# Value products of a fused attention layer: which loop stands innermost

## The reference

```python
q, k, v = split(x @ Wqkv + bqkv)              # 16 heads of 16 channels
scores[.., i] = q[n] . k[n - OFFSETS[i]] * scale + pos_bias[i]
alpha = softmax(scores over the offsets 0..32, 48, 64, 96, 128, 192, 256, 384)
out[n] = sum_i alpha[n, i] * v[n - OFFSETS[i]]
x = layernorm(x + (out * sigmoid(x @ Wgate + bgate)) @ Wout + bout)
```

## Time and profile before

| | before |
|---|---|
| runs, us | 1961.47, 1965.34, 1973.05 |
| median, us | 1965.34 |
| profiled execution, from first to last instruction, us | 1999.0 |
| TensorE busy | 1512.8 us (76%) |
| VectorE, ScalarE, GpSimd busy | 989.1, 905.2, 708.5 us |
| mean granted TensorE clock | 0.797 of full speed |

### The profile page before, as it was taken

One profiled execution on the slowest core, in us unless ns is written; L12 is line 12 of the kernel. 1 busy time (PEld: TensorE's weight loads), 2 busy tenths in 40 slices (PEclk: granted clock), 3 DMA queues, 4 the chain that ended last, 5 costly groups with the idle time before them and its releaser, 6 DMA issues. The chain is left out here.

```text
span 1999.0 us, 72320 instructions
## 1 busy us (share of the span) xinstructions
PE 1512.8 (76%) x31232; PEld 1001.5 (50%) x31232; DVE 989.1 (49%) x2117; ACT 905.2 (45%) x1544; POOL 708.5 (35%) x654
## 2 busy tenths in 40 slices
PE   2447777887778787877778787887875499999970
PEld 1235554555554554545555555555643266776660
DVE  5214455454554455455545455554645355555525
ACT  3123353444435353435445353545443366656626
POOL 6022233433334253333334252433323113323335
PEclk9566786868777797878778787878766699999995
DMA  4483453535243443525242433525210424443328
GB/s 120 91 227 93 88 105 81 112 90 111 76 102 79 88 104 79 116 77 112 64 105 73 88 92 68 110 72 110 57 47 14 140 75 91 101 105 87 72 30 339
DMA packets 220103, 194.55 MB, mean 97 GB/s; under 512 B 66847, under 2 KB 207151, under 8 KB 219648
## 3 DMA queue, kind: packets, MB, share of 16 engines
q1 hardware_dynamic: 204464, 175.11, 35.3%
q0 software_dynamic: 15360, 15.10, 4.7%
HBM read 98.07 MB, written 86.18 MB: 92 GB/s over the span
## 5 line engine op out<-in xcount | busy, mean ns | idle before, releaser
L396 POOL TENSOR_TENSOR p<-p 128x512 f16<-128x512 f32 x96 | 129.0, 1344 | 440.5 <-ACT p L796 427.4
L810 ACT COPY featT<-gp 128x1024 f16<-128x1024 f16 x96 | 93.4, 1032 | 321.3 <-PE gp L541 321.3
L396 DVE TENSOR_TENSOR p<-p 128x512 f16<-128x512 f32 x96 | 94.7, 987 | 284.7 <-ACT p L796 282.8
L548 PE MATMUL gp<-featT,wr 128*128 128x512 f16 x768 | 209.4, 432 | 22.8 <-DVE mT L959 13.8
L1107 POOL DMA_INDIRECT disp<-y,sidx x128 | 174.1, 1360 | 53.6 <-issue 38.0
L1364 POOL DMA_INDIRECT xln<-y,place x64 | 104.9, 1639 | 216.0 <-DVE y L1506 175.7
L1402 PE MATMUL up<-rowsT,w 128*128 128x512 f16 x768 | 171.3, 383 | 9.6 <-DVE w L1479 6.1
L1416 PE MATMUL dn<-w,h 128*128 128x256 f16 x1536 | 170.1, 273 | 0.0
L623 PE MATMUL o<-v_near,p 128*32 128x66 f16 x2048 | 132.3, 203 | 40.0 <-issue 28.4
L795 ACT ACTIVATE p<-st 128x512 f16<-128x512 f32 x192 | 116.7, 608 | 101.0 <-PE st L592 98.1
L1416 PEld LDWEIGHTS dn<-w,h 128*128 128x128 f16 x1536 | 149.7, 98 | 17.3
(11 more groups left out here) (176 smaller groups left out, 3127.0 us busy)
## 6 DMA issues: line engine op xcount, KB each, us to landing
qk_dram<-qk SPq DMA_DIRECT2D x64, 256.0 KB, 2.5
v_near<-vs SPq DMA_DIRECT2D x224, 66.0 KB
qs<-qk_dram SPq DMA_DIRECT2D x96, 128.0 KB, 4.4
ks<-qk_dram SPq DMA_DIRECT2D x96, 128.0 KB, 7.4
o_dram<-o_far SPq DMA_DIRECT2D x64, 136.0 KB, 5.7
o_back<-o_dram SPq DMA_DIRECT2D x16, 544.0 KB, 4.3
v_dram<-vs SPq DMA_DIRECT2D x16, 528.0 KB
v_far<-v_dram SPq DMA_DIRECT2D x64, 132.0 KB
```

The costliest lines, as they stand in the source:

```text
L396: engine.tensor_tensor(p16[:, b, 1, :], p32[:, b, :], p16[:, b, 0, :], ALU.subtract).then_inc(is_split, 1)
L548: last = nc.tensor.matmul(dst, lhs(a, c), rhs(b, c), start=(k == 0), stop=(k == len(todo) - 1))
L810: gp_done(nc.scalar.copy(featT[:, i, :, :].rearrange("f c t -> f (c t)"), bank[:, :].bitcast(F16)), n, stage, PART_OF_T[stage], i)
```

## The change

The loops of the value products are turned inside out: for a pair of heads (z, e) and a term (high or low part of p, with its columns of v), the innermost loop now runs over the four groups of 32 output partitions (near) or over the eight blocks, which are the four groups in each of the two banks (far). Each product keeps its operands, its columns, its bank and its flags, and on one group of partitions the terms of one (z, e) still follow one another in the same order. The count of instructions, the waits at the head and the increment behind the last product stay.

```diff
-                terms3 = ((0, slice(0, OW)), (0, slice(OW, VW)), (1, slice(0, OW)))
-                blocks = [(r8, r8 % 4, 2, 256) for r8 in range(8)] if k < FAR_PAIRS else [(b, b, 4, P) for b in range(4)]
-                for blk, b, groups, width in blocks:
...
-                    for z in range(groups):
                         for e in range(2):
...
-                                nc.tensor.matmul(dst, p(0), v, start=True, stop=False, skip_group_check=True)
-                                last = nc.tensor.matmul(dst[:, :, 0:OW], p(1), v[:, :, 0:OW], start=False, stop=True, skip_group_check=True)
...
+                p = lambda e, a, c: p16[:, 2 * (k % 2) + e, a, c:c + BLOCK]
+                if k < FAR_PAIRS:
+                    for z in range(2):
                         for e in range(2):
+                            for j, (a, cols) in enumerate(((0, slice(0, OW)), (0, slice(OW, VW)), (1, slice(0, OW)))):
+                                for r8 in range(8):
+                                    quad = slice(BLOCK * (r8 % 4), BLOCK * (r8 % 4 + 1))
...
+                                    last = nc.tensor.matmul(dst, p(e, a, 256 * z + BLOCK * r8), v, start=(j == 0), stop=(j == 2), skip_group_check=True)
+                else:
+                    for z in range(4):
+                        for e in range(2):
+                            for a, width in ((0, VW), (1, OW)):
+                                for b in range(4):
+                                    quad = slice(BLOCK * b, BLOCK * (b + 1))
...
+                                    last = nc.tensor.matmul(dst, p(e, a, P * z + BLOCK * b), v, start=(a == 0), stop=(a == 1), skip_group_check=True)
```

More of the change, by code:

```diff
@@ L610, in values @@
                     alone.wait_ge(v_near_in, n.at(256, 256))
-                terms3 = ((0, slice(0, OW)), (0, slice(OW, VW)), (1, slice(0, OW)))
-                blocks = [(r8, r8 % 4, 2, 256) for r8 in range(8)] if k < FAR_PAIRS else [(b, b, 4, P) for b in range(4)]
-                for blk, b, groups, width in blocks:
-                    quad = slice(BLOCK * b, BLOCK * (b + 1))
-                    far = k < FAR_PAIRS
-                    for z in range(groups):
-                        for e in range(2):
[L618 to L622, removed]
-                                nc.tensor.matmul(dst, p(0), v, start=True, stop=False, skip_group_check=True)
-                                last = nc.tensor.matmul(dst[:, :, 0:OW], p(1), v[:, :, 0:OW], start=False, stop=True, skip_group_check=True)
[L625 to L630, removed]
@@ new lines, in values @@
+                p = lambda e, a, c: p16[:, 2 * (k % 2) + e, a, c:c + BLOCK]
+                if k < FAR_PAIRS:
+                    for z in range(2):
+                        for e in range(2):
+                            for j, (a, cols) in enumerate(((0, slice(0, OW)), (0, slice(OW, VW)), (1, slice(0, OW)))):
+                                for r8 in range(8):
+                                    quad = slice(BLOCK * (r8 % 4), BLOCK * (r8 % 4 + 1))
+                                    v = v_far[:, 8 * k + r8, :, :, 2 * z + e, cols].rearrange("p u v c -> p (u v) c")
+                                    dst = o[r8 // 4][:, 0:H * OW].rearrange("q (w h c) -> q w h c", w=4, c=OW)[quad, :, 2 * z + e, 0:cols.stop - cols.start]
+                                    last = nc.tensor.matmul(dst, p(e, a, 256 * z + BLOCK * r8), v, start=(j == 0), stop=(j == 2), skip_group_check=True)
[5 more added lines that the diff above has]
+                                    quad = slice(BLOCK * b, BLOCK * (b + 1))
+                                    v = v_near[:, 4 * (k - FAR_PAIRS) + b, :, 2 * z + e, 0:width]
+                                    dst = o[e][:, 0:PAIRS * VW].rearrange("q (u z c) -> q u z c", u=2, c=VW)[quad, :, z, 0:width]
+                                    last = nc.tensor.matmul(dst, p(e, a, P * z + BLOCK * b), v, start=(a == 0), stop=(a == 1), skip_group_check=True)
```

## The result

The kernel after takes 1944.58 us in the median of eight runs (1936.55 to 1954.96), the kernel before 1962.77 us beside it (eight runs, 1958.3 to 1973.05): ratio 0.9895, 95% interval 0.9866 to 0.9924. It is faster, as forecast and clear of noise, but by 18 us (1%) where 60 were forecast.

What follows compares the result with a forecast made beforehand. TensorE's own order of work was taken to bound a batch. Terms 2.0 + 0 + 1.3 + 0.2 + 0.7 = 4.2 us a batch, 62 us in all, scaled and rounded to 60: 1905 us; range 1860 to 1956.

Steps and rivals of the forecast that it cites:

- The price of a unit: Value products on TensorE: with four groups at once, 8 ns a product, far units 0.88 us, near 0.62, unit 3 0.85.
- the seams: Where one output group's products give way to the next in a unit, they run side by side, 17.5 ns each.
- No overlap: Rival: four interleaved groups don't overlap, or instructions can't come faster than 25 ns a product; 1965 us, chance 0.08.
- two at a time: Lower bound for value units: 17.5 ns a product as at the seams, saving 0.4 us near, 0.7 far.
- Units 0 and 1: Far value products, slots 2 and 4: 3.2 us saved on TensorE, of which 2.0 us a batch reaches the batch's end.
- the y chain: ScalarE's y hangs on the output projection, moves 3 us earlier and carries the far units' gain past the near maxima.
- Absorbed: Rival: the far gain ends in L684's wait, or only two groups run at once; 1935 us, up to 1956, chance 0.20.
- Unit 2, nothing: Near unit in slot 7: its 1.0 us ends in the 4.21 us wait of L684, so nothing is gained.
- Unit 3, 1.3 of 1.55: Near unit in slot 10: 1.3 of 1.55 us saved reaches the batch's end, the rest left to pauses.
- Unit 4, 0.2, and unit 5, 0.7: Near units: 0.2 us a batch for unit 4, whose instructions arrive late; 0.7 instead of 1.0 for unit 5.
- the last sign of being wrong: Wrong on its sizes if pauses without a releaser grow to the amount the products saved, or vanish with them.
- The clock: Rival: denser bursts lower TensorE's granted clock; 0.07 less eats the 62 us, 0.13 less gives 2015 us; chance of slower 0.05.

Runs made afterwards that it cites:

- before_again: The unchanged kernel before, run and profiled a second time: 1960.44 us, ratio 0.9995 to the kernel before.
- short_stack: The kernel after with the last of three loads of each stacked q and k half cut to one row (scores left wrong): 1915.2 us, 0.9761 of before.
- far_only: The kernel before with the new order in the far units 0 and 1 only: 1956.11 us, 0.9979 of before.
- near_only: The kernel before with the new order in the near units 2 to 5 only: 1951.61 us, 0.9958 of before.
- warm_both: The kernel after with 12 idle products a batch ahead of the stacks' wait and 15 ahead of the output projection's wait: 2002.27 us, 1.0185 of before.
- near_high: The kernel after without the near units' low-part products (32 instead of 64 a unit): 1887.78 us, 0.9634 of before.
- after_lead128: The kernel after with 64 tiny products (128 instructions) run once ahead of the loop over batches: 1958.9 us, 0.9991 of before.
- warm_stack: The kernel after with 12 idle products of 512 columns a batch ahead of the wait for the stacks: 1975.52 us, 1.006 of before.

## Why the prediction was off

**The price of a unit: right.** Forecast 0.88, 0.88, 0.62, 0.85 us for units 0 to 3; measured 0.92, 1.0, 0.82 and 0.82 in the mean of ten batches (unit 2 at half the clock, which is why it isn't 0.62). Four groups do run at once, and the mechanism of the seams was the right row to read. The sentence of the Trainium skill that a weight load overlaps running products only if the row groups differ ("TensorE: Matmul & The Clock Gate", Part 3, What overlaps and what doesn't) does not hold here, with one row group and 8.3 ns a product; "No overlap" and the "two at a time" bound are out. TensorE's busy time fell by 100 us over the execution (1500.2 to 1400.3 us on the pages of `before_again` and after), at the upper end of the 80 to 100 forecast.

**Units 0 and 1, "I take 2.0": this step failed.** The prediction had the right row in hand, L684 with 0.15 us of slack to the stacks, and let the y chain carry 2.0 of the 3.2 us past it. In the trace of after that line (now L683) waits 2.8 us a batch for `ks`, where it waited 0.3. The rows that answer to 938.76 and 949.01 of the earlier trace rows:

```profile
827.15 0.39 PE L683 MATMUL gp<-near_bias,sel_rest 32*128 32x512 f16 x2 [2.42 <-DMA ks<-qk_dram]
...
835.54 0.60 PE L683 MATMUL gp<-near_bias,sel 32*128 32x512 f16 x2 [0.80 <-DVE m_near L965]
```

The wait for `m_near` did shrink, 4.25 to 3.15 us a batch, as the y chain said, but the stall put unit 2 and its scores at 0.50. The windows from the output projection to the far maxima in one batch, before and after:

```profile
829.85:850.09 20.24, 13.28 (x427) 9.11 (x428) 13.62 (x36) 5.07 (x9) 3.92 (x6) 0.67 0.48 122
```

```profile
819.95:840.63 20.68, 13.65 (x426) 8.76 (x427) 13.23 (x36) 5.08 (x9) 3.93 (x6) 0.58 0.67 142
```

The whole stretch is no shorter (20.24 and 20.68 us) at 0.58 for 0.67 of the clock, and this batch is a mild one: the mean of ten is 20.2 us before, 21.9 after and 19.9 in `short_stack`. Measured from the head of the batch, TensorE of after is 2.96 us ahead of before where the output projection starts, 0.67 where the near maxima start, and 1.04 at the next head; in `short_stack` it is 2.94, 3.54 and 4.05. `far_only` kept 0.7 us a batch of 3.07; `short_stack` shows that it is the stacks: with them in time the new order is 3.0 us a batch faster. "Absorbed" named the place rightly and got 0.20; I judged by one batch of an untypical execution, the one with the longest `m_near` wait of ten. The measured time lies within that rival's 1935 to 1956 us, but not by its sum: it let units 3 and 5 keep 2.0 us, and most of that went to pauses.

**Unit 2, nothing: right in the result.** It saved 1.03 us (1.85 to 0.82), its scores grew by 0.62 (1.80 to 2.42), and in `near_only` the wait for `m_near` grew instead (42.5 to 46.8 us in ten batches).

**Unit 3, 1.3 of 1.55: failed.** The rest was "left to pauses like those of unit 4"; the pauses took nearly all: unit 3 saves 1.59, the scores behind it grow 1.63 (`near_only`: 1.49).

**Unit 4, 0.2, and unit 5, 0.7.** The units saved 0.97 and 0.62 us, but the far scores behind unit 5 grew 0.91 (2.66 to 3.57) and the pauses ahead of the far maxima's products 0.45 (12.7 to 17.2 us in ten batches). "A faster burst only starts the pauses earlier" was written for unit 4 alone, and the row it rested on was of another kind: in that execution units 4 and 5 have 33 pauses over 0.3 us in the ten batches, from 0.3 to 8.2 us behind the start of the last transfer of instructions. As a mechanism it fits what the other units' scores did. It should have been a term of every near unit: there were 22.5 us of inner pauses in the old order too. It stood as the last sign of being wrong only, and that sign came true by half: pauses without a releaser grew by 33.5 us where the products saved 75.

**The clock.** Forecast as a rival that needs -0.07; it fell 0.06 (0.78 to 0.72), and TensorE's other work took 21 us more in ten batches, some two thirds of what that rival priced (0.07 for 3.9 us a batch; at most 2.1 for 0.06). The work beside the units did not stay dense. About half of the fall is the stacks' wait: `short_stack` takes it away and has 0.75. The rest is not: `near_only`, with 2.7 us of that wait in ten batches, stands at 0.73, with the denser near units and 46.0 us of inner pauses. What part of it the pauses cause was not separated; some is only that less time at 1.00 goes into the mean. Raising the clock by filler (`warm_both`) gained nothing.

**The sum.** 4.2 us a batch forecast, 1.0 measured in the steady batches: the two terms that failed are the 2.0 us of units 0 and 1, which went to the stacks, and pauses after units 3 and 5, which stood at next to nothing and took about as much as these units saved. By alignment the same edit is worth other amounts: 0.9895 with no lead, 0.9991 / 1.0262 = 0.974 with 128 instructions ahead. There the kernel before has 50 us of inner pauses too; at the alignment that was forecast it stands well, with 22.5. How the profiled execution of 1999.0 us came to its pauses in units 4 and 5 stays open: one execution shows them. So does what makes one alignment dearer than another.

## What to carry to other kernels

Rotate small products over the groups of output partitions: 64 products take 0.66 us instead of 1.63. But before that is counted as time, find the arrival that next holds TensorE (here DMAs with 0.15 us of slack) and move it with the change. When bursts of products get dense, count instructions as well as cycles: compare two versions of a kernel at more than one alignment of their code before a difference of 1 or 2% is ascribed to the edit, and profile a kernel twice if its span lies outside its runs.

## What the runs showed of the hardware

TensorE's instructions arrive in transfers of 16 KB, 256 instructions each (16 transfers less for 4096 instructions less in `near_high`). Products that pause in the middle of a stage go on about 2.4 us after the start of such a transfer (48 pauses in after). These stops stand at the same products in every turn of the loop, and n instructions ahead moved them n/2 products earlier, to within one (`after_lead128`, `warm_stack`). Sixty-four products of 8 columns, run once, cost the kernel before some 50 us (1.0262), and twelve products of 512 columns a batch, put into a wait that was idle anyway, cost the one after 32 us (1.006 against 0.9895). Groups of output partitions work side by side: 64 near products start in 0.66 us when they rotate over four groups and in 1.63 us when 16 in a row write one (`before_again`). The old order had fewer stops at one of two alignments only (22.5 and 50.1 us in ten batches).
